# Relation edge stage of a two-layer graph network: the one-hot built on VectorE and transposed on TensorE, q and peak sent through it as bf16 parts, the score split on GpSimd

## The reference, cut to what matters

```
k, q, v = typed_linear(x, ...)              # 6250 x 4 heads x 64
att = (q[edge_dst] * k_rel[edge_type, edge_src]).sum(-1) * rel_pri / sqrt(64)
seg = edge_dst * 6 + edge_type              # 37,500 segments
amax = segment_max(att, seg)
ex = exp(att - amax[seg]);  denom = segment_sum(ex, seg)
hsum = segment_sum(ex / denom[seg] * val_e, seg)     # then mean over relations
```

## Time and profile before

| | |
|---|---|
| median of 3 runs | 4749.34 us (4734.86 to 4750.56) |
| profiled execution, first to last instruction | 4737.6 us |
| what lies around it (median less span) | 11.7 us, 0.25% |
| busy over the span | PE 85%, DVE 87%, ACT 61%, POOL 71% |
| chunks in `edges_1` | 312 |

### The profile page before, as it was taken

How to read it: one execution, slowest core, us unless ns; L and a number is a source line. 1 busy time by engine, 2 the same in 40 slices (tenths; PEclk the granted TensorE clock), 3 DMA queues, 4 the chain that set the end, 5 groups by cost and what they waited for, 6 DMA issues and landing times. The chain is left out here.

```text
span 4737.6 us, 112614 instructions
## 1 busy us (share of the span) xinstructions
PE 4031.9 (85%) x23408; PEld 3334.4 (70%) x23408; DVE 4120.2 (87%) x13250; ACT 2900.4 (61%) x8405; POOL 3352.1 (71%) x3818
## 2 busy tenths in 40 slices
PE   0778888888888878999799898999999898968887
PEld 0357777777777767899677777777777677757776
DVE  6779999999999995555599999999999999968887
ACT  0765555555555543333488888888888888862222
POOL 0568888888888861111488888888888888857776
PEclk9989999999999998999888888888888888879899
DMA  2568777777777775666577777777777777776664
GB/s 75 179 206 250 229 228 228 228 228 227 228 229 228 228 190 174 202 200 197 168 207 206 204 206 204 206 204 205 205 204 206 204 204 204 205 158 189 176 170 133
DMA packets 647755, 950.12 MB, mean 201 GB/s; under 512 B 215768, under 2 KB 490760, under 8 KB 647287
## 3 DMA queue, kind: packets, MB, share of 16 engines
q0 software_dynamic: 153600, 510.70, 38.4%
q1 hardware_dynamic: 494043, 438.22, 32.1%
HBM read 777.56 MB, written 171.03 MB: 200 GB/s over the span
## 5 line engine op out<-in xcount | busy, mean ns | idle before, releaser
L1385 POOL DMA_INDIRECT kv1c<-kv_table,rec x936 | 916.8, 980 | 305.5 <-issue 175.2
L741 POOL DMA_INDIRECT kv<-kv_table,rec x864 | 921.3, 1066 | 247.3 <-issue 241.8
L1439 ACT ACTIVATE wv<-kv1c,wv 128x64 f32<-128x64 f32 x3744 | 927.7, 334 | 2.1
L1517 DVE CUSTOM_DVE_ANT_0 masked_scores<-score_p,mask 126x384 f32<-126x384 f32 x1248 | 679.5, 545 | 11.4 <-issue 5.8
L1615 PE MATMUL sum_p<-wv,hot 128*126 128x260 f32 x1872 | 626.3, 482 | 2.3 <-ACT wv L1439 2.3
L908 PE MATMUL sum_p<-msg,hot 128*126 128x256 f32 x1728 | 433.6, 394 | 192.2 <-DVE msg L864 192.2
L1577 PE MATMUL qe_p<-qrel,hotT 126*128 126x256 f32 x1872 | 546.9, 436 | 21.0 <-ACT hotT L1417 14.2
L1374 POOL TENSOR_SCALAR hot<-iota,local 128x126 f32<-128x126 f32 x936 | 549.7, 600 | 0.3 <-issue 0.2
L908 PEld LDWEIGHTS sum_p<-msg,hot 128*126 128x126 f32 x1728 | 309.4, 189 | 280.5 <-DVE msg L864 213.2
L1577 PEld LDWEIGHTS qe_p<-qrel,hotT 126*128 126x128 f32 x1872 | 428.8, 229 | 108.2 <-ACT hotT L1417 14.4
L1615 PEld LDWEIGHTS sum_p<-wv,hot 128*126 128x126 f32 x1872 | 398.4, 228 | 89.8 <-ACT wv L1439 2.7
(11 more groups left out here) (222 smaller groups left out, 10254.0 us busy)
## 6 DMA issues: line engine op xcount, KB each, us to landing
key<-segment_keys SPq DMA_DIRECT2D x312, 189.0 KB
q_blk<-q_table SPq DMA_DIRECT2D x216, 192.5 KB
acc_table<-acc SPq DMA_DIRECT2D x312, 128.0 KB
qrel<-q_by_relation SPq DMA_DIRECT2D x312, 126.0 KB
acc_in<-acc_table SPq DMA_DIRECT2D x50, 767.8 KB
q_by_relation<-qrel SPq DMA_DIRECT2D x50, 756.0 KB
feat<-in_edge_feat_t SPq DMA_DIRECT2D x216, 128.0 KB
agg_table<-total SPq DMA_DIRECT2D x216, 126.0 KB
```

The source lines that it names most:

```text
L741: pool.indirect_dma_start(kv[k][:, t, :], None, c["kv0_d"], bass.IndirectOffsetOnAxis(ap=rec[k][:, t, 0:1].bitcast(I32), axis=0)).then_inc ...
L1385: pool.indirect_dma_start(kv[k][:, t, :], None, c["kv1_d"], bass.IndirectOffsetOnAxis(ap=rec[k][:, t, 0:1].bitcast(I32), axis=0)).then_inc ...
L1439: ins = act.activation(wv[k][:, t, h, 0:DK], kv[s][:, t, D + h * DK:D + (h + 1) * DK], ACT.Copy, scale=wv[k][:, t, h, DK:DK + 1])
L1517: dve.tensor_tensor_reduce(junk[k][:, h, :], score_p[:, h, :], mask[it.slot(4)][:], 1.0, -BIG, ALU.add, ALU.max, top[s][:, h:h + 1]).then_ ...
```

## The change

The one-hot is compared once, on DVE: `hot` = (iota + block base == key), one operation of 378 elements a row. PE transposes it (`turn_hot`, three transposes into the new PSUM tile `hotT_p`), ACT copies it out as bf16 (`transposed_hot`) and makes the mask from the same PSUM tile. The `key` load, `distances`, `locate` and POOL's compares are gone.

With a bf16 hotT, q comes as three bf16 parts (`Q1_ROW` = 768): `q_of_edges` has 9 bf16 products in place of 3 float32 ones. `nodes_1` makes the parts: ACT copies all three PSUM tiles to bf16, DVE subtracts, ACT copies the remainder (1536 wide), POOL subtracts (1536 wide). The peak is split too: four small DVE operations (`peak_part`) at the end of DVE's list, three bf16 products with 12 columns on PE, and a DVE reduction (`peak_back`) at the head of DVE's list that adds the parts up. `cap` is gone. The score split moves to POOL, in its list between the first and the second gather, and `fade_acc` now stands behind the second gather. `spread` has 6 products with up to 384 columns in place of 12 with 128.

```diff
@@ POOL's list
-                run_chunks(pool, steps, ((5, fade_acc), (1, one_hot), (0, gather)))
+                run_chunks(pool, steps, ((0, gather((0,))), (2, lead_part(0)), (2, rest_part(0)), (2, lead_part(1)),
+                                         (2, rest_part(1)), (0, gather((1,))), (5, fade_acc), (0, gather((2,)))))
@@ POOL
+                def lead_part(j):
+                    def f(it):
+                        k = it.slot(2)
+                        if j == 0:
+                            hold(pool, held, score_ready, it.count())
+                            wait(pool, partsT_turned, it, 2)
+                            pool.sem_inc(held, 1)
+                        else:
+                            hold(pool, held, split_ready, it.count(1, 4, 2 * j))
+                        src = score[it.slot(4)] if j == 0 else rest[k][j - 1]
+                        pool.tensor_copy(parts[k][:, :, j, :], src[:]).then_inc(split_ready, 1)
@@ ACT's list
-                run_chunks(act, steps, ((1, transposed_hot), (2, masks), (0, distances), (4, weights), (2, partsT_out)))
+                run_chunks(act, steps, ((4, weights), (1, transposed_hot), (4, values(0)), (1, masks), (4, values(1)),
+                                        (2, partsT_out), (4, values(2))))
@@ DVE
+                def one_hot(it):
+                    s = it.slot(U)
+                    wait_slot(dve, loaded, it, LOADS)
+                    wait(dve, summed, it, U)
+                    dve.scalar_tensor_tensor(
+                        hot[s][:], c["iota"][:].rearrange("p (o n) -> p o n", o=1).to_broadcast([P, T1, SEG]),
+                        par[s][:, 0:1], rec[s][:, :, 2:3].to_broadcast([P, T1, SEG]),
+                        ALU.add, ALU.is_equal).then_inc(hot_ready, 1)
+                def peak_part(j):
+                        if j == 0:
+                            wait(dve, peak_ready, it)
+                            wait(dve, spread_back, it, 2)
+                            dve.tensor_scalar(peak_parts[k][:, 0, :], peak[s][:], 1.0, None,
+                                              ALU.mult).then_inc(peak_split, 1)
...
+                def peak_back(it):
+                    wait(dve, spread_back, it)
+                    wait(dve, diff_ready, it, 2)
+                    dve.tensor_reduce(of_edge[it.slot(2)][:], peak_p.rearrange("p t (j h) -> p t h j", j=PARTS),
+                                      AX, ALU.add).then_inc(of_edge_ready, 1)
@@ DVE's list
-                run_chunks(dve, steps, ((2, q_times_k), (4, below_peak), (2, scores), (4, cap), (0, locate),
-                                        (3, maxima(0)), (2, lead_part(0)), (3, maxima(1)), (2, rest_part(0)),
-                                        (3, maxima(2)), (2, lead_part(1)), (3, maxima(3)), (2, rest_part(1)),
-                                        (3, old_peak), (5, add_acc), (3, new_peak), (3, peak_drop)))
+                run_chunks(dve, steps, ((4, peak_back), (2, q_times_k), (4, below_peak), (2, scores), (3, old_peak),
+                                        (0, one_hot), (3, maxima(0)), (3, maxima(1)), (3, maxima(2)), (3, maxima(3)),
+                                        (5, add_acc), (3, new_peak), (3, peak_drop), (3, peak_part(0)),
+                                        (3, peak_part(1)), (3, peak_part(2)), (3, peak_part(3))))
@@ PE
+                def turn_hot(it):
+                    wait(pe, hot_ready, it)
+                    wait(pe, mask_ready, it, 1)
+                    for t in range(T1):
+                        ins = pe.transpose(hotT_p[:, t * P:(t + 1) * P], hot[it.slot(U)][:, t, :], c["ident"][:])
+                    ins.then_inc(hotT_turned, 1)
 
                 def peaks_of_edges(it):
                     k = it.slot(4)
-                    wait(pe, peak_ready, it)
-                    wait(pe, diff_ready, it, 1)
+                    wait(pe, peak_split, it, per=4)
+                    wait(pe, of_edge_ready, it, 1)
@@ PE's list
-                run_chunks(pe, steps, ((5, sum_values), (1, q_of_edges), (2, turn_parts), (3, peaks_of_edges),
-                                       (2, spread)))
+                run_chunks(pe, steps, ((5, sum_values), (1, turn_hot), (1, q_of_edges), (2, turn_parts),
+                                       (3, peaks_of_edges), (2, spread)))
```

261 lines of the change are left out of this document (129 added, 132 removed).

## The result

| | before | after |
|---|---|---|
| median | 4745.14 us (4734.86 to 4750.56) | 5419.3 us (5406.16 to 5423.66) |
| profiled span | 4737.6 us | 5416.1 us |
| mean granted clock over the span | 0.925 | 0.858 |

The ratio is 1.1421, 95% interval 1.1401 to 1.1441: 14% slower. The forecast was 5078 us with a range of 4840 to 5300. The direction was right; the size was not, and the time lies outside the range. One execution of experiment 10's kernel took 12473 us, far from its other three, and is left out of its ratio.

A forecast was written before the change was run, and what follows sets the result against it. POOL was taken to set 6.12 us a chunk; a new DVE-POOL-PE loop would make it 7.15. 4737.6 + 321 (edge stage) + 7 (nodes_1) = 5066 span, 5078 us median, 8-in-10 range 4840 to 5300.

The forecast's parts named there:

- Everything else ... cost nothing: Edge stage: the other edits, on ACT, PE and DMA, have slack under 7.15 us a chunk and add 0.
- 2.05 + 3.04 + 1.53 + 0.53 = 7.15: Edge stage: closed loop through DVE, POOL and PE sets 7.15 us a chunk, 1.03 over 6.12, +321 us.
- Leg A: Edge stage, DVE from the start of `peak_back` to the score ready: 2.05 us.
- Leg B: Edge stage, POOL from the score through the four split operations and a gather to `faded` ready: 3.04 us.
- Leg C: Edge stage, DVE's tail from `faded` ready through `acc`, `peak` and `drop` to the last peak part: 1.53 us.
- Leg D: Edge stage, PE's three peak products and pick-up, until DVE's next `peak_back` starts: 0.53 us.
- 4.5 ... that cover would still be wide: Edge stage, PE: 3.6 to 3.7 us work at full clock plus 0.8 waiting for ACT's hotT copy, under 7.15.
- POOL is the engine that sets the pace: Edge stage before the change: POOL's operations and issue gaps sum to 6.12 us, equal to the measured chunk pace.
- Rival 2: Edge stage: DVE's `one_hot` and `peak_part` collide with POOL, adding 0.45 us; pace 7.6, 5218 us; chance 0.14.
- Rival 3: Edge stage: PE all at 1.2 GHz, pace 8.1 us a chunk, 5374 us; chance 0.07.
- Rivals 1, 4 and 5: Edge stage: only peak's round trip stays, 4837 us (0.15); both trips hide, 4672 us (0.04); no change (0.03).

The follow-up runs named there:

- experiment 10: Kernel of experiment 3 with `partsT_out` ahead of `values(1)` in ACT's list: 5349.9 us, ratio 1.1084; repeated on another chip 5280.2 us, 1.1134.
- experiment 1: Changed kernel with 104 one-column DVE memsets ahead of the edges_1 loop, moving its start from instruction 2041 to 2145: 5236.5 us, ratio 1.1038.
- 2: Kernel before with 34 such memsets, so its edges_1 loop starts at the changed kernel's place, 2041: 4814.7 us, ratio 1.0149.
- 4: Experiment 1 with `one_hot` moved behind the fourth maxima in DVE's list: 5209.7 us, ratio 1.0983.
- 7: Changed kernel with one peak part in place of three, `peak_part(1)` to `(3)` left out: 5136.0 us, ratio 1.0830.
- 13: Experiment 1 with `fade_acc` directly behind the split in POOL's list, ahead of the second gather: 4977.7 us, ratio 1.0498.
- 3: Experiment 1 with `fade_acc` at the head of POOL's list, ahead of gathers and split: 5098.5 us, ratio 1.0735.
- experiment 8: Changed kernel with the score split back on DVE, `fade_acc` then gather on POOL, `old_peak` behind the maxima, no memsets: 5281.1 us, ratio 1.1141.
- experiment 14: Experiment 3 with 3 bf16 products in place of 9 in `q_of_edges`: 5376.4 us, ratio 1.1334.
- experiment 6: Kernel before with one DVE `one_hot` compare replacing `locate` and POOL's three compares, plus 26 memsets: 4743.6 us, ratio 1.0001.
- 15: Experiment 14 with six unused products of 384 columns on PE ahead of its wait for `partsT_ready`: 5383.7 us, ratio 1.1361.
- 16: Experiment 13 with four unused products of 256 columns on PE ahead of its wait for `hotT`: 4950.7 us, ratio 1.0453.

## Why the prediction was wrong, by its own steps

*"Everything else ... cost nothing"* is the step that failed most. The change shifted DVE's loop from instruction 2007 to 2041, across an edge of what is fetched. That is 183 us of the 341 by which the median missed (experiments 1, 2), and the loop of nodes_out, moved from 3008 to 3051, gave 22 us back. Neither was a term of the sum, nor a rival. The kernel before had the sign of it: a 2.9-us gap in each iteration of nodes_out, and instruction packets as a queue of their own. The Trainium skill (page "Runtime: NRT & Kernel Launch", section "Instruction fetch mechanics") says that a taken branch whose target is outside the fetched window stalls until it is fetched. The trace agrees, with 0.3 us inside and 3 to 5 us outside. The section's figure, two pages of 256 instructions, the runs don't bear out. By it the starts at which such a loop fits would make one stretch modulo 256; but going round 256, 97 fits (start 2145), 192 stalls (3008), 235 fits (3051) and 249 stalls (2041). Modulo 128 every start that fits lies from 82 to 107, and none that stalls does, so the period looks like 128.

*The chain, "2.05 + 3.04 + 1.53 + 0.53 = 7.15"*: found rightly, each wait where it was said, and 7.69 long.

- Leg A 2.13 in place of 2.05 (`of_edge` 0.19 to its follower, not 0.11).
- **Leg B, 3.53 in place of 3.04**, the mis-sized term: the pick-up 0.27 (0.16), the four operations with their gaps 1.33 (1.12; 0.21 rather than 0.20 each, but the first 0.38), the gather's gap 0.30 (0.16).
- Leg C 1.70 in place of 1.53: pick-up 0.19, the first peak part 0.30.
- Leg D 0.33 in place of 0.53: 3 products of 12 columns in 0.23, and no pick-up worth the name. The 0.20 too many here hid as much of what the other legs lacked.

That makes 0.54 us a chunk, 168 us. One chunk is shown, but the others are like it: over 283 chunks of experiment 1 the median legs are 2.14, 3.52, 1.71 and 0.33. Experiments 4, 7 and 13 took 0.19, 0.58 and 1.28 us out of the chain, and 0.09, 0.36 and 0.83 came off the pace. The traces show where the rest went: legs A to C fall by what was taken out (B to 3.34 in 4, C to 1.11 in 7, B to 2.21 in 13), and the mean of leg D, DVE's wait for PE, grows from 0.39 to 0.44, 0.62 and 0.80. That the chain sets the pace of the changed kernel is shown; that nothing else is near it, is not so.

*The second chain.* The slack given to PE, "4.5 ... that cover would still be wide", was a sum of PE's own work at full clock. The loop that PE is in has ACT's list in it, and is 6.18 us at full clock and 8.38 at half. In the changed kernel, at 0.73, it lies on both sides of 7.69, and I put to it what experiment 1 has beyond the chain, 0.05 us a chunk or 17 us; it lies in leg D. In 7 and 13 it is what ate the gain, in 3 and 8 together with the stretched small operations; in 14 it is the pace.

The terms together, against the forecast span of 5066: +181 branch (0.58 us a chunk between the changed kernel and experiment 1, of which the gaps themselves are 167), +168 chain, +17 second chain, +8 in the later start, -22 nodes_out, 5418; the span is 5416.

*What bounds the kernel now, "POOL is the engine that sets the pace"*: not shown by the rows, and wrong if it means POOL alone (experiment 6). In the chunk read there POOL had no wait, but DVE and PE were nearly full beside it, and their operations were not added up in the same way. Once POOL's compares were gone, `capped` fell from a mean of 425 ns to 171, so part of DVE's load was POOL's doing. The error did not enter the sum, which starts from the measured 6.12.

*The rivals.* Rival 2 (DVE and POOL hinder each other) is true at the places named: `one_hot` against the first split, and the first peak part. It was worth 0.19 + 0.13, not 0.45. The Trainium skill's rule (page "SBUF — State Buffer", section "Who interferes with whom"), two SBUF inputs on DVE against GpSimd, fits `one_hot`, beside which the cast ended only when `one_hot` had. The first peak part has one SBUF input, but it is a `tensor_scalar`, and the same section says that this operation can enter modes that use two ports and then contends too. The trace agrees as far as durations go (0.61 us beside `faded` in experiment 8, 0.17 alone); in which mode it ran, no run shows. Rival 3 (half clock, 8.1) is not this kernel but experiment 14. Rivals 1, 4 and 5 fell with the two waits. Nodes_1 cost nothing, as said: 39.93 us an iteration in both traces. The range failed because all its cases were chains; none was a cost outside the lists.

Open: what grants the clock. In 14 work was taken from PE and it was 0.62 and not 0.80; in 15 products were added and it stayed at 0.62; in 16 it was 0.88 and not 0.84. Open too is what exactly bounds edges_1 before, and how long the second chain lay above the first in the changed kernel. No run puts back the changed kernel's parts one at a time beyond 6, 7 and 8, so what `nodes_1` and the wider q rows cost is read from the traces alone.

## What to carry to other kernels

Look for a gap of microseconds marked "issue" at the first operation behind a loop's branch, and for the instruction queue's packets: any edit ahead of a loop can move it across a fetch edge, and moving it by some small operations tells this cost from the edit's own, here 183 us of 674. Give each engine's list its own closed loop, with the waits of the others in it and at both clock levels; a slack reckoned from an engine's busy time is not one. Before moving an operation up a list, ask what its own wait will hold back.

## What the runs showed of the hardware that was not expected

- A loop of 337 to 340 DVE instructions stalls 3 to 5 us at its branch (2, 25, 64, 121) or not at all (82 to 107), by its start modulo 128. At 64 a second gap of 3.7 to 5.6 us follows a few instructions on. An iteration that stalls fetches five packets of 8.2 KB.
- Taking two thirds of a matmul step away went with a granted clock of 0.62 in place of 0.80 and 294 us more; four products of no use in idle time went with 27 us less.
- A POOL operation of 12 elements a row takes 0.19 to 0.21 us, and a gather begins 0.30 us behind such an operation and 0.16 behind `faded` (0.24 in experiment 8).
- A 4-element DVE operation takes 0.17 us alone. It ends with `faded` when it starts beside it (0.6 us), and with a gather when it starts 0.3 to 0.5 us before the gather's end; with 0.7 us of the gather left it isn't held up.
